# Two changes to a decoder layer: the gate's high and low columns in one stationary operand, and a reordered last feed-forward

## The reference

```
x = layernorm(x + attention(x))          # 16 heads of 32, causal, biases
x = layernorm(x + wkv(x, ctx))           # keys are x, values ctx_2048; a recurrence over 256 tokens per channel
x = layernorm(x + ffn(x))
```

```
gating = softmax(x @ W_gate.T)           # 16 gate columns
idx = argmax(gating);  top1 = max(gating)
q, k, v = split(x @ W_qkv.T)
k_shared = k of head idx;   v_shared = top1 * v of head idx
y = softmax(causal(q_h k_shared^T / sqrt(32))) v_shared, for each of 16 query heads h
```

## Time and profile before

| | us |
|---|---|
| median of 3 executions | 1458.68 (1454.87 to 1460.93) |
| the profiled execution | 1456.15 |
| its span | 1454.3 |
| TensorE matmul busy | 1386.3 (95%) |
| VectorE busy | 1089.8 (75%) |
| ScalarE busy | 649.3 (45%) |
| GpSimd busy | 380.3 (26%) |

### The profile page before, as it was taken

The page is one execution under the profiler, slowest core; times in us unless marked ns, Lnnn a source line. Parts: engine busy times, 40 slices in busy tenths (PEclk is TensorE's granted clock), DMA queues, the critical chain, the costliest instruction groups (busy, mean ns, idle before and its releaser), DMA issues.

```text
span 1454.3 us, 26609 instructions
## 1 busy us (share of the span) xinstructions
PE 1386.3 (95%) x9908; PEld 1109.4 (76%) x9908; DVE 1089.8 (75%) x2258; ACT 649.3 (45%) x1459; POOL 380.3 (26%) x520
## 2 busy tenths in 40 slices
PE   7887999999999999999999999999999999999895
PEld 6675778878787887878788787777877777787663
DVE  5366777787887788778777877877887877779863
ACT  3543535445352544545254454525445353454233
POOL 1245322322232232223223322322322232232200
PEclk9899999999999999999999999999999999999997
DMA  6531423314243331424333141433314243330120
GB/s 180 170 88 45 96 81 85 100 33 113 55 96 96 85 99 37 112 52 95 96 85 100 43 111 47 96 96 85 99 35 100 66 96 95 74 95 17 44 60 30
DMA packets 63199, 119.50 MB, mean 82 GB/s; under 512 B 14304, under 2 KB 32736, under 8 KB 63072
## 3 DMA queue, kind: packets, MB, share of 16 engines
q1 hardware_dynamic: 60128, 112.03, 30.6%
q10 hardware_dynamic: 2944, 5.77, 1.2%
HBM read 32.81 MB, written 8.39 MB: 28 GB/s over the span
## 4 chain that ended last, share of the span: by engine, by line
PE 76%; SPq 5%; DVE 5%; ACT 2%; issue 1%; DMA 1%; POOL 0%; ACTq 0%; POOLq 0%; DVEq 0%
PE pp L486 8%; PE pp L488 8%; PE pp L487 8%; PE po L591 7%; PE pw L486 5%; PE pw L488 5%; PE pw L487 5%; SPq L318 4%; PE sk L511 4%; PE sq L511 3%; PE sq L532 3%; PE po L595 3%; PE po L605 3%; PE sq L526 3%; PE sk L564 3%; PE sk L574 2%
## 5 line engine op out<-in xcount | busy, mean ns | idle before, releaser
L1529 DVE TENSOR_REDUCE neg_max<-sq 128x2 f32<-128x512 f32 (+1 forms) x384 | 252.3, 684 | 116.3 <-PE sq L511 115.2
L1163 ACT ACTIVATE prob<-sk 128x512 f32<-128x512 f32 x384 | 215.8, 597 | 231.0 <-PE sk L511 226.4
L486 PE MATMUL pp<-xt_hi,w_hi 128*128 128x256 f32 x616 | 188.6, 306 | 12.1 <-DVE w_lo L1516 7.4
L488 PE MATMUL pp<-xt_hi,w_lo 128*128 128x256 f32 x616 | 175.2, 284 | 0.0
L487 PE MATMUL pp<-xt_lo,w_hi 128*128 128x256 f32 x616 | 175.1, 284 | 0.0
L1174 ACT ACTIVATE o_ch<-po 128x512 f32<-128x512 f32 x128 | 76.4, 597 | 158.4 <-PE po L595 157.0
L2050 POOL TENSOR_TENSOR w_ev<-w_e,w_val 128x256 f32<-128x256 f32 x64 | 46.0, 719 | 353.7 <-ACT w_e L1220 322.2
L486 PEld LDWEIGHTS pp<-xt_hi,w_hi 128*128 128x128 f32 x616 | 119.6, 194 | 14.3 <-issue 10.7
L511 PE MATMUL sq<-mask_qk,ident_b 128*128 128x256 bf16 (+1 forms) x384 | 124.4, 324 | 0.0
L511 PE MATMUL sk<-mask_kq,ident_b 128*128 128x256 bf16 (+1 forms) x384 | 123.9, 323 | 0.0
L487 PEld LDWEIGHTS pp<-xt_lo,w_hi 128*128 128x128 f32 x616 | 119.2, 194 | 0.3
(11 more groups left out here) (203 smaller groups left out, 3667.6 us busy)
## 6 DMA issues: line engine op xcount, KB each, us to landing
q_stack<-q_hi SPq DMA_DIRECT2D x256, 128.0 KB, 2.4
q_stack<-q_lo SPq DMA_DIRECT2D x128, 128.0 KB, 2.5
k_stack<-k_hi SPq DMA_DIRECT2D x128, 128.0 KB, 2.3
x_raw<-in_xT SPq DMA_DIRECT2D x16, 512.0 KB, 3.8
k_stack<-k_lo SPq DMA_DIRECT2D x64, 128.0 KB, 2.3
x<-in_x SPq DMA_DIRECT2D x16, 512.0 KB, 4.3
w_val<-in_ctxT SPq DMA_DIRECT2D x64, 128.0 KB, 2.2
out_y<-x SPq DMA_DIRECT2D x13, 512.0 KB, 3.0
```

The lines of the kernel that those rows point to most:

```text
L486: T.matmul(out, lh, rh, start=(c == 0), stop=False, skip_group_check=True)
L488: mm = T.matmul(out, ll, rh, start=False, stop=(c == CC - 1), skip_group_check=True)
L1163: A.activation(dst, sk[n % 2][:], ACT.Exp, scale=SCALE).then_inc(s_exp, 1)
L1529: V.tensor_reduce(dst, src, AX.X, ALU.max, negate=True).then_inc(s_max, 1)
```

## The change

1. `gate_hi` and `gate_lo` become two halves of one tile `gate_both`. For each chunk one matmul with all 32 columns against `xt_hi` gives hi·hi in `pw[0:16]` and lo·hi in `pw[16:32]`, and a second one adds hi·lo to `pw[0:16]`. `gate_out` copies 32 rows, and `gating` adds the two halves after the transpose.
2. In the feed-forward of the last batch, groups 1 and 3 write their exponentials to `w_key` and `w_e1` (tiles 0, 1) and `w_d` (tile 2), groups 0 and 2 to `prob0` and `w_ev`. These four are tiles of the recurrence, which is over by then. The order of all engines in that part is changed, and six `keep` matmuls are put ahead of `values_f` in groups 1, 2 and 3.
3. `third_norm(n)` and `store_whole(n)` move behind the last `copy_f(b, 3)`; for this VectorE's last `third_stats` waits for `ln_biased`, and GpSimd's last `inverse_std` for `x3_ready`.

```diff
-F_LINKS, F_LINK_K3, F_LINK_PICKED = 25, 11, 15
+F_LINKS, F_LINK_K3, F_LINK_PICKED = 26, 12, 16
...
+        gate_both = sb("gate_both", [P, CC, 2, NH], f32r)
+        gate_hi, gate_lo = gate_both[:, :, 0, :], gate_both[:, :, 1, :]
...
+        def prob_early(b, g, k, last_f):
+            if last_f and is_last(b) and g % 2:
+                return (w_key, w_e1)[k // 2][:, k % 2, :]
+            return prob0[:, k, :]
...
+        def prob_late(b, g, last_f):
+            if last_f and is_last(b):
+                return (w_ev, w_d)[g % 2][:].rearrange("p c t -> p (c t)").rearrange("p (h q) -> p h q", h=HG)
+            return prob1[:]
...
-                products(pw[0:NH, 0:S], lambda c: (gate_hi[:, c, :], gate_lo[:, c, :]), tokens(0, S)).then_inc(u_job, 1)
+                for c in range(CC):
+                    T.matmul(pw[0:2 * NH, 0:S], gate_both[:, c, :, :].rearrange("p a h -> p (a h)"), xt_hi[:, c, :],
+                             start=(c == 0), stop=False, skip_group_check=True)
+                    mm = T.matmul(pw[0:NH, 0:S], gate_hi[:, c, :], xt_lo[:, c, :],
+                                  start=False, stop=(c == CC - 1), skip_group_check=True)
+                mm.then_inc(u_job, 1)
...
                 pe.wait_ge(f_exp, TILES * b)
+                sk_f(b, 0, 0, 1)
+                max_f(b, 1)
+                sq_f(b, 2, 0, 1)
+                sk_f(b, 0, 2)
+                sq_f(b, 2, 2)
                 for g in range(NG):
-                    sk_f(b, g, 0, 1)
-                    if g:
-                        turn_f(b, g - 1)
                     if g + 1 < NG:
-                        max_f(b, g + 1)
+                        sk_f(b, g + 1, 0, 1)
                     if g + 2 < NG:
-                        sq_f(b, g + 2, 0, 1)
-                    sk_f(b, g, 2)
-                    if g + 2 < NG:
-                        sq_f(b, g + 2, 2)
+                        max_f(b, g + 2)
                     if g == 0:
                         wait_links_f(pe, b, F_LINK_PICKED + 1)
                         pe.wait_ge(f_norm, NG * b)
+                    else:
+                        keep(pp, 6)
                     values_f(b, g)
-                turn_f(b, NG - 1)
+                    if g + 3 < NG:
+                        sq_f(b, g + 3, 0, 1)
+                    if g + 1 < NG:
+                        sk_f(b, g + 1, 2)
+                    if g + 3 < NG:
+                        sq_f(b, g + 3, 2)
+                    turn_f(b, g)
...
                 exps_f(b, 0, 2)
-                copy_f(b, 0)
                 exps_f(b, 1, 0, 1)
                 row_hi_f(b, 2)
+                copy_f(b, 0)
                 exps_f(b, 1, 2)
+                exps_f(b, 2, 0, 1)
+                row_hi_f(b, 3)
                 copy_f(b, 1)
+                exps_f(b, 2, 2)
+                exps_f(b, 3, 0, 1)
+                copy_f(b, 2)
+                exps_f(b, 3, 2)
+                copy_f(b, 3)
                 third_norm(n, x_of(n))
                 store_whole(n)
-                exps_f(b, 2, 0, 1)
-                row_hi_f(b, 3)
-                exps_f(b, 2, 2)
-                copy_f(b, 2)
-                exps_f(b, 3, 0, 1)
-                exps_f(b, 3, 2)
-                copy_f(b, 3)
                 third_norm(b, x_of(b))
...
-                V.tensor_copy(logit_t[0:NH, :], pw[0:NH, 0:S]).then_inc(u_free, 1)
+                V.tensor_copy(logit_t[0:2 * NH, :], pw[0:2 * NH, 0:S]).then_inc(u_free, 1)
...
-                V.tensor_copy(logit[:], pw[:, 0:TT * P].rearrange("p (c h) -> p c h", c=TT)[:, :, 0:NH]).then_inc(u_free, 1)
+                parts = pw[:, 0:TT * P].rearrange("p (c h) -> p c h", c=TT)
+                ch.link(V.tensor_copy(logit[:], parts[:, :, 0:NH]))
+                V.tensor_tensor(logit[:], logit[:], parts[:, :, NH:2 * NH], ALU.add).then_inc(u_free, 1)
...
                 maxima_f(b, 0, 0, 1)
                 gate_value(chf, b)
+                maxima_f(b, 0, 2)
                 pick_value(chf, b, 0)
-                maxima_f(b, 0, 2)
                 rows_f(b, 0)
                 maxima_f(b, 1, 0, 1)
                 pick_value(chf, b, 1)
                 maxima_f(b, 1, 2)
                 rows_f(b, 1)
                 maxima_f(b, 2)
+                rows_f(b, 2)
+                maxima_f(b, 3)
                 third_residual(chf, b, 0, x_of(b))
-                rows_f(b, 2)
+                rows_f(b, 3)
                 third_stats(n, x_of(n))
-                maxima_f(b, 3)
                 third_residual(chf, b, 1, x_of(b))
-                rows_f(b, 3)
```

More of the change, by code:

```diff
@@ L86, in build @@
                                ("w_raw", [P, NW, CC, D], f32, 0))
-        gate_hi = sb("gate_hi", [P, CC, NH], f32r)
-        gate_lo = sb("gate_lo", [P, CC, NH], f32r)
+        gate_both = sb("gate_both", [P, CC, 2, NH], f32r)
+        gate_hi, gate_lo = gate_both[:, :, 0, :], gate_both[:, :, 1, :]
         q_stack = sb("q_stack", [P, NH, S], f32r)
@@ L299, in wait_links_f, with prob_pair @@
             eng.wait_ge(s_f, F_LINKS * at + n)
+        def prob_early(b, g, k, last_f):
+            if last_f and is_last(b) and g % 2:
+                return (w_key, w_e1)[k // 2][:, k % 2, :]
+            return prob0[:, k, :]
+        def prob_pair(b, g, i, last_f):
+            if last_f and is_last(b) and g % 2:
+                return (w_key, w_e1)[i][:]
+            return prob0[:, 2 * i:2 * i + 2, :]
+        def prob_late(b, g, last_f):
+            if last_f and is_last(b):
+                return (w_ev, w_d)[g % 2][:].rearrange("p c t -> p (c t)").rearrange("p (h q) -> p h q", h=HG)
+            return prob1[:]
         def values_done(b):
@@ L586, in values @@
                 pe.wait_ge(s_exp, TILES * b + 3 * (g + 1))
+                late = prob_late(b, g, s_exp is f_exp)
                 for pair in range(HG // 2):
@@ L590, in values @@
                         k = 2 * pair + j
-                        T.matmul(po[VW * j:VW * j + HD + 1, at:at + S], value(0, HG * g + k), prob0[:, k, :],
+                        T.matmul(po[VW * j:VW * j + HD + 1, at:at + S], value(0, HG * g + k), prob_early(b, g, k, s_exp is f_exp),
                                  start=True, stop=False, skip_group_check=True)
@@ L594, in values @@
                         k = 2 * pair + j
-                        mm = T.matmul(po[VW * j:VW * j + HD + 1, at + P:at + S], value(1, HG * g + k), prob1[:, k, :],
+                        mm = T.matmul(po[VW * j:VW * j + HD + 1, at + P:at + S], value(1, HG * g + k), late[:, k, :],
                                       start=False, stop=True, skip_group_check=True)
@@ L1159, in exps @@
                     if i < 2:
-                        dst = prob0[:, 2 * i:2 * i + 2, :].rearrange("p h q -> p (h q)")
+                        dst = prob_pair(b, g, i, s_exp is f_exp).rearrange("p h q -> p (h q)")
                     else:
-                        dst = prob1[:].rearrange("p h q -> p (h q)")
+                        dst = prob_late(b, g, s_exp is f_exp).rearrange("p h q -> p (h q)")
                     A.activation(dst, sk[n % 2][:], ACT.Exp, scale=SCALE).then_inc(s_exp, 1)
@@ L1383, in opening @@
                 qk_hi(0, PA_K + 1)
-                A.activation(gate_hi[:], gate, ACT.Copy).then_inc(gate_split, 1)
+                A.activation(gate_hi, gate, ACT.Copy).then_inc(gate_split, 1)
                 A.activation(decay[:], decay[:], ACT.Exp).then_inc(act_once, 1)
@@ L1726, in third_stats @@
                 ch.n = F_LINKS - 1
+                if is_last(b):
+                    dve.wait_ge(ln_biased, b)
                 ln_stats(ch, 2, x)
@@ L1871, in opening @@
                 dve.wait_ge(gate_split, 1)
-                V.tensor_tensor(gate_lo[:], gate, gate_hi[:].bitcast(f32), ALU.subtract)
+                V.tensor_tensor(gate_lo, gate, gate_hi.bitcast(f32), ALU.subtract)
                 dve.wait_ge(act_once, 2)
@@ L2156, in ending @@
                 third_bias(r)
+                pool.wait_ge(x3_ready, LAST)
                 inverse_std(LAST, 2)
```

## The result

| | before | after |
|---|---|---|
| median of 10 executions, us | 1457.94 (1454.87 to 1461.52) | 1449.25 (1444.38 to 1452.45) |
| the profiled execution, us | 1456.15 | 1448.82 |
| its span | 1454.3 | 1447.0 |

The ratio is 0.9943, with a 95% interval of 0.993 to 0.9955: 8.3 us less (6.6 to 10.2), where 12.5 were forecast. The time lies in the range and the sign is right, but the forecast saving is half as large again as the measured one.

What follows compares the result with a forecast made beforehand. TensorE was taken to bound the loop, latency and order the last feed-forward. Gate 6.9 plus tail 5.6 gave 12.5 us, taken from a median of 1458.68 for 1446.2, forecast as 1446 us, range 1440 to 1452.

Steps and rivals of the forecast that it cites:

- What it no longer has to issue should come off the span: Loop: TensorE waits for nearly nothing, so four fewer gate matmuls save 0.45 us a batch, 6.3 us over 14 gates.
- Rival B: Gate: another chain, with SyncE's late DMA queue as evidence, sets the period, so its loop saving is lost; 1452.4 us, chance 0.11.
- Weight loads of 32 columns: Gate: 16 more columns per load might cost 13 ns each, 0.8 us over 16 batches if nothing hid it.
- Rival C: Gate: VectorE's added operation with its link holds up TensorE each batch; slower, 1465.7 us at 1.4 us a batch, chance 0.05.
- The two last gates: Gates of batches 14 and 15: 0.22 us saved on the first, the full 0.45 us on the second.
- The tail, 5.6 us: Last feed-forward: the new order starts group 3's values at 1437.05 in place of 1442.62, 5.6 us earlier.
- Rival A: Last feed-forward: TensorE's clock still falls to half rate in holes; tail gives 2.1 to 3.9, 1447.9 to 1449.7 us, chance 0.14.
- The same length behind group 3's values: End of the last feed-forward: copy, turn, residual, statistics and norm keep their length; a collision with the store costs under 1 us.
- `third_norm(n)` off the path, 1.98 us: Last feed-forward: ScalarE's norm and store issue, 1.98 us on the path, move beside the last turn, residual and statistics.
- The hiccup of SyncE's queue: Loop: a 1.3 us delay once per iteration, left where it is since SyncE's program is unchanged; might fall elsewhere, 1 us an iteration.

Runs made afterwards that it cites:

- gate_five: The changed kernel with three more gate matmuls left out (hi times lo only for the last chunk); ratio 0.994 to the kernel before, periods 84.30 to 84.34 us.
- add_only: The kernel before with only the link and the addition put into the gating, all twelve gate matmuls kept; ratio 0.9997 to the kernel before.
- gate_only: The kernel before with only the gate's part of the change (gate_both, gate_out, gating); ratio 0.9975 to the kernel before, 3.6 us less.
- norm_back: The changed kernel with third_norm and the store of batch 14 put back behind the copy of group 1; ratio 0.9976 to the kernel before.

## Why the prediction was right in the tail and wrong in the gate

- **"What it no longer has to issue should come off the span"** is the step that failed. 0.45 us a batch was right to the hundredth, and 6.3 us for the loop was not: 14 x 0.14 = 2 us arrived by the periods. All in all the gate was put at 6.9 us and brought 3.6 (2.2 to 5.0) by its own ratio. From busy shares of 86.79 in 87 us I took it that TensorE has no co-bound. I priced the wait that the change adds, and never asked of each wait ahead of which TensorE would now arrive sooner how close it already was. The transpose of maxima had too little slack. Two rows of the trace before bound it: `k_lo` ended at 265.59 and the transpose started at 265.85, so it was 0.26 us at most, where the sum needed 0.45. With the 0.15 that the release costs, 0.11 was left.
- **Rival B** had the mechanism in general form (another chain sets the period), but named the wrong chain: SyncE's keys, where it was VectorE's scans. Its price, 1452.4, left out the 2 us. What the Trainium skill says there ("Perfetto Trace Analysis", section "Identifying the Most-Contended Engine"), that matmul busy time is no good measure, fits this case: after the change TensorE is still busy for 86.56 of 87 us (263 to 350), and `gate_five` gains nothing from three matmuls less.
- **Weight loads of 32 columns**: they are hidden; the pace stayed at 0.113.
- **Rival C**, the added operation: 0 us, as taken. The two last gates: for batch 15 it is 17.89 to 17.90 us from the gate to the keys' copy in the three traces with twelve gate matmuls, and 17.42 to 17.54 in seven of the eight with eight, so that 0.35 to 0.48 arrived, as the 0.45 of the forecast. Only the first trace of the changed kernel has 17.69. For batch 14 there is nothing to be told.
- **The tail, 5.6 us**: 5.4 us by the tail's own ratio (3.2 to 7.4). In the two traces that were first compared it was 4.14, but the old order took 33.66 us in one trace, 35.08 in `add_only` and 35.16 in `gate_only`, and the new one 29.03 to 29.82 in the six traces that have it unchanged: 5.2 between the means (34.63 and 29.41). That this is near 5.6 is in part luck, as two errors cancel. The new order was forecast at 28.09 (1408.96 to 1437.05) and took 1.3 more: the steps of 5.76, 4.27 and 3.68 us were put at 5.0, 4.1 and 3.1. The first of them was mis-sized most, in TensorE's own work, without a wait. The old order took 1.0 more than in the one trace that the forecast was made from. Up to the values of group 3 it had two half-rate stretches there; in the other two traces of the same order it had a third one of 3.4 us, and the step from group 2 to group 3 took 5.76 and 5.82 us in place of 4.36. What decides whether the third one comes, no run here shows. In the new order there is one half-rate stretch in each of the six traces, as in the forecast, so Rival A did not happen. The windows at that step, first in `add_only`, then in the kernel before:

```profile
1435.60:1439.00 3.40, 3.19 (x17) 1.80 (x17) 0.00 (x0) 0.44 (x2) 0.00 (x0) 0.50 0.01 2
```

```profile
1438.00:1441.40 3.40, 3.10 (x25) 2.04 (x25) 0.14 (x1) 1.65 (x4) 0.00 (x0) 1.00 0.01 2
```

- **The same length behind group 3's values**: 11.7 us to the end before, 11.8 after, so the store that was moved cost nothing that can be seen.
- **`third_norm(n)` off the path, 1.98 us**: putting it back cost about 5, since the clock falls during the wait. The gain of an order without this hole is more than the hole.
- **The hiccup of SyncE's queue** was said to stay where it is. It did not: the long periods are mostly the 9th to 13th in the three traces with twelve gate matmuls; in those with eight the main run of them begins at the 4th or 5th. SyncE's program is the same, so its place depends on something else; what, no run here shows. The link that the prediction read holds after the change too: in the 5th period (85.69 us) the same issues take 2.42 us where they take 1.08 an iteration before, and TensorE then waits for the keys. SyncE's queue, then TensorE:

```profile
496.67 1.08 SPq L352 DMA_DIRECT2D w_val<-in_ctxT  x2
...
581.01 2.42 SPq L352 DMA_DIRECT2D w_val<-in_ctxT  x2
```

```profile
584.47 0.63 PE L544 MATMUL sq<-k_stack,q_stack 96*128 96x128 f32 x4 [0.92 <-DMA k_stack<-k_lo]
```

## What to carry to other kernels

A busy share of 99% says what an engine does, not that nothing stands right behind it. When work is taken off such an engine, walk forward from there and read, at each wait of the engine, by how much the releaser was early. If the releaser does not wait for the work that was taken off, the smallest of these is about what arrives. Here it was 0.11 us for a change worth 0.45, and 0.14 arrived.

Where the clock of TensorE depends on what it did before, a wait costs its length and then the slow work behind it: in `norm_back` 2.89 us of wait came to 5.3.

## What was not expected

The hiccup of SyncE's queue (about 1.3 us, about once per iteration) moves the long periods, and with them 3 us of a single execution between the two traces of the changed kernel, so two profiles of one kernel differ by a third of what this change is worth. The first gate, at 175.3 to 181.4 us in the twelve traces, moves it by up to 6 us more. Between two profiles, only stretches of the same kind can be compared: clean periods with clean periods, from the same mark to the same mark.
